# A fused cross-attention and ternary FFN kernel: the order of the first scale, of the token transposes and of one FFN tile on TensorE

## The reference, cut to what matters

```
act_quant(x)  : scale = 127 / max(|x|) per token;  round(x*scale) / scale
bit_linear    : act_quant(x) @ ternary(w).T
FFN           : h = bit_linear(x, w1)          256 -> 1024
                h = silu(depthwise_conv1d(h))  3 taps along the tokens
                y = bit_linear(h, w2)          1024 -> 256
```

## Time and profile before

| | us |
|---|---|
| median of 3 runs | 1536.86 |
| lowest and highest run | 1536.23, 1538.49 |
| profiled execution, its own time | 1535.5 |
| span of the profile, first to last instruction | 1533.5 |
| busy: TensorE / its weight loads | 1409.5 / 1159.5 |
| busy: VectorE / ScalarE / GpSimd | 1195.5 / 1182.3 / 668.1 |

### The profile page before, as it was taken

One profiled execution on the slowest core, in us unless ns is written; L12 is line 12 of the kernel. 1 busy time (PEld: TensorE's weight loads), 2 busy tenths in 40 slices (PEclk: granted clock), 3 DMA queues, 4 the chain that ended last, 5 costly groups with the idle time before them and its releaser, 6 DMA issues.

```text
span 1533.5 us, 33070 instructions
## 1 busy us (share of the span) xinstructions
PE 1409.5 (92%) x10604; PEld 1159.5 (76%) x10650; DVE 1195.5 (78%) x3059; ACT 1182.3 (77%) x3909; POOL 668.1 (44%) x1058
## 2 busy tenths in 40 slices
PE   7899999999999999999999999999999999999762
PEld 4688778787777878777787878788787777878541
DVE  4363698787969878796887878688787878788888
ACT  3477787978878797887879788787978788797832
POOL 2354444445444444544544454444445444444420
PEclk9999999999999999999999999999999999999985
DMA  9210100000010100000010000001000000100000
GB/s 279 53 31 16 31 16 28 20 28 30 24 34 15 33 11 28 30 28 29 15 44 1 29 28 28 29 15 44 8 23 28 28 29 15 44 1 1 29 15 14
DMA packets 41144, 47.13 MB, mean 31 GB/s; under 512 B 3024, under 2 KB 35216, under 8 KB 41104
## 3 DMA queue, kind: packets, MB, share of 16 engines
q1 hardware_dynamic: 41104, 46.62, 10.1%
HBM read 36.13 MB, written 10.49 MB: 30 GB/s over the span
## 4 chain that ended last, share of the span: by engine, by line
PE 43%; DVE 30%; ACT 17%; issue 9%; DMA 1%; DVEq 0%; POOL 0%; SPq 0%; POOLq 0%; ACTq 0%
PE PS L500 10%; ACT SM L751 8%; PE PS L462 6%; PE PS L443 5%; PE PS L513 5%; PE PS L478 4%; PE PS L487 4%; PE PS L452 3%; PE PS L591 2%; DVE HP L1003 2%; DVE GBS L1062 2%; DVE MX L914 2%; DVE GBS L1086 2%; DVE HP L1009 2%; ACT QM L719 2%
## 5 line engine op out<-in xcount | busy, mean ns | idle before, releaser
L1238 POOL TENSOR_TENSOR SM<-SM,RC 128x496 f32<-128x496 f32 (+1 forms) x512 | 324.2, 654 | 738.6 <-DVE RC L908 738.6
L751 ACT ACTIVATE SM<-PS,MX 128x124 f32<-128x124 f32 x1024 | 359.9, 367 | 159.1 <-DVE SM L916 155.8
L500 PE MATMUL PS<-KT,QM 128*128 128x128 f32 x2048 | 278.1, 279 | 24.0 <-ACT SM L751 24.0
L500 PEld LDWEIGHTS PS<-KT,QM 128*128 128x128 f32 x2048 | 249.4, 192 | 38.6 <-ACT SM L751 38.1
L751 ACT ACTIVATION_READ_ACCUMULATOR SM<-PS,MX 128x1 f32 x1024 | 212.2, 207 | 0.0
L1269 POOL TENSOR_TENSOR OTl<-OF,OTh 128x256 fp32r<-128x256 f32 x256 | 204.1, 797 | 10.4 <-ACT OF L745 10.4
L487 PE MATMUL PS<-IDF,SM 128*128 128x128 f32 x1024 | 168.4, 287 | 16.6 <-POOL SM L1238 16.5
L743 ACT ACTIVATE OTh<-PS 128x256 fp32r<-128x256 f32 x256 | 100.4, 392 | 93.5 <-PE PS L478 92.5
L914 DVE TENSOR_REDUCE MX<-PS 128x4 f32<-128x496 f32 x256 | 170.5, 666 | 0.4 <-issue 0.4
L478 PEld LDWEIGHTS PS<-PT,V 128*64 128x64 f32 x2048 | 106.6, 136 | 82.3 <-issue 75.4
L478 PE MATMUL PS<-PT,V 128*64 128x128 f32 x2048 | 168.6, 286 | 0.0
(11 more groups left out here) (166 smaller groups left out, 3511.5 us busy)
## 6 DMA issues: line engine op xcount, KB each, us to landing
XIN<-in_x SPq DMA_DIRECT2D x16, 512.0 KB, 3.5
XRES<-in_x SPq DMA_DIRECT2D x16, 512.0 KB, 4.6
out_y<-HP SPq DMA_DIRECT2D x15, 512.0 KB, 3.2
CRAW<-in_ctxT SPq DMA_DIRECT2D x16, 256.0 KB, 2.7
RRAW<-in_ctxT SPq DMA_DIRECT2D x32, 128.0 KB, 2.9
QM<-in_Wq SPq DMA_DIRECT2D x1, 1024.0 KB, 9.1
GBS<-in_Wo SPq DMA_DIRECT2D x1, 1024.0 KB, 14.0
k_ipa_columns<-HP SPq DMA_DIRECT2D x1, 1024.0 KB, 6.5
```

Of the source, the lines that this page charges most:

```text
L500: m = mm(psS[:, h, :], QM[:, 2 * q + h // 2, h % 2, TOK * b:TOK * b + TOK], KT[:, 2 * q + h // 2, b, :], start=True, stop=True)
L751: m = act.activation(SM[s % 2][:, h, 0:ORG], psS[:, h, 0:ORG], ACT.Exp, bias=MX[s % 2][:, h:h + 1], accum_out=SU[s % 2][:, h:h + 1])
L1238: m = pool.tensor_tensor(part, part, RC[c % 2][:, 4 * i:4 * i + 4].unsqueeze(2).broadcast_to(shape), ALU.mult)
```

## The change

The scale's transposes (L582) move from half 14 to half 12, ahead of the transposes of the tokens (L576), and ScalarE's copy to BC with them, from half 15 to half 13. The waits are exchanged to fit: the scale's transposes now wait for `fin_done`, the tokens' transposes for `bc_done`, tile 0 for `q1t_done`. Separately, in half 16 TensorE runs the FFN step (tile 1) ahead of the projections (a V unit) instead of behind them.

```diff
-M_QT, M_BC1 = 13, 14
+M_QT, M_BC1 = 13, 12
...
+M_AHEAD = (16,)
...
                 if n == M_QT:
                     pe.wait_ge(q1_done, g.count(1, 1))
-                    need(pe, fin_done, g.count(2, 0))
+                    pe.wait_ge(bc_done, g.count(1, 1))
...
                 if n == M_BC1:
                     pe.wait_ge(scale_done, g.count(2, 1))
-                    pe.wait_ge(q1t_done, g.count(1, 1))
+                    need(pe, fin_done, g.count(2, 0))
...
                     if j == 0:
-                        pe.wait_ge(bc_done, g.count(1, 1))
+                        pe.wait_ge(q1t_done, g.count(1, 1))
...
+                if n in M_AHEAD and g.shift(-1).exists():
+                    finish(g.shift(-1), n)
                 if g.exists():
                     project(g, n + HALVES)
...
-                if g.shift(-1).exists():
+                if n not in M_AHEAD and g.shift(-1).exists():
                     finish(g.shift(-1), n)
```

## The result

The changed kernel takes 1539.22 us (median of 19 runs, 1538.10 to 1541.33) against 1536.20 us for the kernel before (19 runs, 1534.88 to 1538.49). The ratio is 1.0021, with a 95% interval from 1.0015 to 1.0027: slower by 3 us, a little more than the 0.2% that can be told from no change. The forecast was 1535.8 and no change; 1539.2 lies inside the range. The profiled execution took 1539.69 us with a span of 1537.7, against 1535.5 and 1533.5 before.

The account below looks back on a forecast made before the run. The kernel was taken as bound by hand-overs between nearly full engines. 15 x (2.12 - 0.35 - 0.78 - 1.06) = -1.05 us from the profiled 1535.5 gives 1534.4, as median 1535.8; range 1532.4 to 1539.9.

Parts of the forecast that it names:

- Part 1: Transposes and BC copy moved earlier: half 14's scores 2.12 us later; after 0.35 and 0.78 back, half 16's P times V +0.99.
- Part 2: Half 16, tile 1 ahead of the V unit: tile 2 need not wait for VectorE, giving back 1.06 us per group.
- ScalarE's lateness, the first rival: Tile 1's gate in half 19: ScalarE over 0.59 us late delays VectorE, up to 0.40 per group, 1541.9 us; chance 0.24.
- the first and the last taken as the others: Sum over the loop: all 15 groups counted alike at -0.07 us each, -1.05 us in all.
- by the rows the clock adds nothing to the sum: New wait at the tokens' transposes, about as long as an old 1.7 us wait with clock 1.00: no cost.
- rival of the falling clock: Halves 14 to 16 up to tile 2 at 1.2 GHz after the new wait: +150 us, 1687; chance 0.02.
- The period that was named as a sign, near 88.6: Changed profile, one loop pass: near 88.6 us if right; wrong if off 88.70 by over 0.2.
- the slip of 88.70: One loop pass was taken as 88.70 us, only the stretch cut out; copy to copy it is 89.00.

Follow-up runs that it names:

- part 1 alone: Changed kernel with tile 1 behind the V unit again, so only the transposes and BC copy move: 1552.13 us, ratio 1.0098.
- part 2 alone: Kernel before, with only tile 1 moved ahead of the V unit in half 16: 1522.72 us, ratio 0.9905.
- filler run: Changed kernel with six unread 512-column matmuls put ahead of the tokens' transposes in the last pass: 1536.49 us, ratio 0.9998.
- e5: Kernel before, with ScalarE's BC copy ahead of the projection's copies in half 15, TensorE's lists untouched: 1525.45 us, ratio 0.9926.
- e7: Changed kernel, with ScalarE's BC copy in half 12 ahead of that half's exponentials: 1514.50 us, ratio 0.9856.

## Why the prediction was right and wrong

**Part 1, right.** The path through ScalarE's exponentials and the copy ends where it was said to: the copy starts directly behind the exponentials, and P times V of half 14 is 804.75 - 800.04 = 4.71 behind the start of VectorE's last output, against 2.01 before: 2.70 later (forecast 2.63). The scores are 2.19 later (2.12), P times V of half 16 1.04 (0.99). The run with part 1 alone gives +1.06 for a pass. The 0.05 to 0.07 too little is in the hand-over from the copy to the tokens' transposes: the copy ends at 804.07, the transposes start at 804.22, where 0.05 was taken. This is read from the trace; no run tested it.

**Part 2, right in kind, a tenth too much.** Tile 2's wait is gone, VectorE follows the tile as foretold, and the run with part 2 alone gives -0.90 (forecast -1.06). Of the missing 0.16, 0.12 is a reading error. The prediction had the tile start 2.57 behind P times V, where the V unit now begins; but that row is a weight load. The V unit's first matmul stands 0.12 behind it in the timeline of before:

```profile
811.53 0.28 PE L462 MATMUL PS<-WVh,CTh 128*128 128x256 f32 x1
```

So from P times V to the next matmul it is 2.69, and tile 1 starts just so (810.53 to 813.22). With the 0.05 of part 1 this turns -0.07 into +0.10 per pass; +0.12 was measured.

**ScalarE's lateness, the first rival: it did not come.** VectorE's gate (L1012, 822.54) starts without a wait, and at 830.58 ScalarE still waits 1.11 for VectorE (1.14 before). Costing this at nothing was right.

**The step that failed** is "the first and the last taken as the others", and with it "by the rows the clock adds nothing to the sum". The prediction compared the length of the new wait in the loop, 1.47, with the longest old one, 1.7, found the clock at 1.00 there, and closed the case. It never worked out how long the new wait is in the last pass. The terms were there. The wait in the loop lies behind a V unit of 1.28 us; in the last pass no projection is left, so the wait had to be 1.47 + 1.28 = 2.75 (measured 2.51), longer than any row had shown to be harmless. The rival of the falling clock was therefore real. It was priced as if it would strike all 15 passes or none (+150), and it struck one, for 2.4 us by the filler run. The kernel before had a row that spoke for it: in this same pass a tile waits 2.27 us for VectorE, and behind that wait the granted clock is at 0.50 (rows in the last section). (What the prediction calls the last group's tile 0 is that of the last group but one, in this pass.)

The Trainium skill, "TensorE: Matmul & The Clock Gate", in the section "Why this matters for your kernels", warns of long gaps between bursts of matmuls. This trace agrees: behind the wait of 2.51 us the clock is at 0.50. The row that was held against this warning covered a shorter gap than the one that the change made.

**The sum.** The terms of the loop missed by about as much as the last pass. The forecast took 0.07 off each pass; the passes up to the last one added 1.30 in all. The mis-sized terms are the two above: 2.57 for the 2.69 from P times V to tile 1, and 0.05 for the 0.15 from the copy to the tokens' transposes. The 1.30 and the 2.28 of the last pass make 3.6 us; the two spans differ by 4.2, the medians by 3.0. Without the clock's fall, the changed order takes as long as the kernel before as far as these runs can tell (filler run, 0.9998). That 1539.2 lies between 1532.4 and 1539.9 is in part luck: this range was made of hand-overs in equal passes and held nothing for the last one. The period that was named as a sign, near 88.6, carried the slip of 88.70; against the 89.01 of before, +0.12 is within the 0.2 that it allowed.

## What to carry to other kernels

When a wait moves, work out its length in every copy of the loop body, the prologue and the drain above all: the work that covers it in the loop may be missing there. A wait behind another engine is best looked for in that engine's own order: here one call moved on ScalarE (e5, e7) gave what the reordering on TensorE was meant to give and did not. And where two edits come as one, run each alone; this change was a gain of 0.95% and a loss of 0.98%.

## What was not expected of the hardware

A wait of 2.51 us in which TensorE did nothing, behind a stretch with 0.62 us of matmuls in 3.3, was followed by more than 5 us at the 1.2 GHz level (granted clock 0.50), and it cost 2.4 us. In the loop, and for tile 0 in the last pass, waits of 1.37 to 1.67 us were followed by a clock of 1.00. Six matmuls that nobody reads, 1.65 us of work put into the gap, kept the clock up and made the program faster than the changed kernel without them.

The length of a wait alone does not tell whether the clock falls. Later in the last pass a tile waits 2.27 us for VectorE in either kernel. First the kernel before, the matmuls that end the wait and the busy time by window behind them, then the changed one:

```profile
1441.63 0.61 PE L591 MATMUL PS<-Q1T,W 128*128 128x512 bf16 x2 [2.27 <-DVE GBS L1062]
...
1442.50:1445.50 3.00, 3.00 (x20) 2.67 (x15) 3.00 (x5) 2.72 (x8) 0.86 (x1) 0.50 0.00 0
```

```profile
1445.25 0.60 PE L592 MATMUL PS<-Q1T,W 128*128 128x512 bf16 x2 [2.27 <-DVE GBS L1065]
...
1445.25:1449.25 4.00, 3.93 (x33) 2.94 (x36) 4.00 (x5) 3.84 (x13) 1.73 (x2) 1.00 0.00 0
```

In the kernel before the clock is at 0.50 behind this wait, in the changed one at 1.00. A little later in the changed kernel, a wait of only 1.65 us (up to 1456.70) is followed by 0.50. What decides between them stays open: no run here varied the work around a wait at a fixed length.
